# A graph network on one core: the last edge pass with masked scans in place of selection products

## The reference

```python
h = jnp.maximum(_layernorm(x, axis=-1), 0.0)
x = x + _L3_gnn_ref(h, edge_index, ...)

def _L3_gnn_ref(x, edge_index, W_e, b_e, W_n1, b_n1, W_n2, b_n2):
    src, dest = (edge_index[0], edge_index[1])
    edge_in = jnp.concatenate([x[src], x[dest]], axis=1)
    edge_attr = jax.nn.relu(edge_in @ W_e + b_e)            # 256 wide
    msg = jax.nn.relu(jnp.concatenate([x[dest], edge_attr], axis=1) @ W_n1 + b_n1)   # 256 wide
    agg = jax.ops.segment_sum(msg, dest, num_segments=x.shape[0])
    return jax.nn.relu(agg @ W_n2 + b_n2)                   # 128 wide
```

## Time and profile before

| | us |
|---|---|
| median of 3 runs | 3399.61 (3371.57 to 3420.72) |
| profiled execution, span from first to last instruction | 2778.5 |
| profiled execution, its own time | not listed apart from the three runs |
| `phase_mlp` in the span | from about 2110 to the end |

### The profile page before, as it was taken

The page is one execution under the profiler, slowest core; times in us unless marked ns, Lnnn a source line. Parts: engine busy times, 40 slices in busy tenths (PEclk is TensorE's granted clock), DMA queues, the critical chain, the costliest instruction groups (busy, mean ns, idle before and its releaser), DMA issues. The chain is left out here.

```text
span 2778.5 us, 52641 instructions
## 1 busy us (share of the span) xinstructions
PE 2088.4 (75%) x11015; PEld 1440.1 (52%) x11015; DVE 1937.7 (70%) x8744; ACT 1827.5 (66%) x4630; POOL 1430.0 (51%) x1442
## 2 busy tenths in 40 slices
PE   3376666676764888849884899566664999999996
PEld 1154444444443777748884544233332666666663
DVE  8687777777774777768885788688884555555552
ACT  4498888787884888869993343799992444444442
POOL 7777777777765666367770000000003566666663
PEclk9789988988897999979996999899997999999998
DMA  2355565565653666556661542799994222222220
GB/s 77 93 172 185 182 186 178 164 189 173 183 159 101 169 169 170 155 145 196 198 195 53 148 127 82 217 306 308 307 300 138 60 70 78 77 79 83 76 72 23
DMA packets 457630, 419.73 MB, mean 151 GB/s; under 512 B 56299, under 2 KB 353974, under 8 KB 457460
## 3 DMA queue, kind: packets, MB, share of 16 engines
q1 hardware_dynamic: 391028, 343.53, 40.5%
q0 software_dynamic: 64192, 74.09, 10.4%
q10 hardware_dynamic: 2240, 0.01, 0.0%
HBM read 236.96 MB, written 184.33 MB: 152 GB/s over the span
## 5 line engine op out<-in xcount | busy, mean ns | idle before, releaser
L2313 POOL DMA_INDIRECT mlp_bx<-t_X,k_bslot x2 | 2.0, 1016 | 609.0 <-POOLq L2579 608.7
L2329 POOL DMA_INDIRECT out_dram<-mlp_ou,mlp_iro x200 | 200.5, 1002 | 185.7 <-issue 185.4
L486 POOL DMA_INDIRECT second_xs<-t_X,second_irs x200 | 199.7, 999 | 126.9 <-ACT second_m L1227 50.8
L2322 POOL DMA_INDIRECT mlp_xs<-t_X,mlp_irs x200 | 202.5, 1012 | 72.9 <-issue 60.0
L486 POOL DMA_INDIRECT a_xs<-in_x_dram,a_irs x200 | 206.4, 1032 | 61.4 <-issue 58.8
L486 POOL DMA_INDIRECT first_rd<-t_R,a_irs x200 | 202.8, 1014 | 66.9 <-issue 59.7
L486 POOL DMA_INDIRECT project_xs<-t_X,project_irs x200 | 199.8, 999 | 65.8 <-issue 63.3
L2383 DVE TENSOR_TENSOR mlp_v<-mlp_ps_r,mlp_b 126x512 f32<-126x512 f32 x50 | 34.6, 692 | 243.0 <-ACT mlp_y L2442 233.2
L2205 PE MATMUL x_ps_o<-x_ht,x_wd 128*128 128x512 f32 (+1 forms) x198 | 115.8, 668 | 96.3 <-DVE x_ht L2105 79.7
L2485 PE MATMUL mlp_ps_e<-mlp_h,mlp_we 128*128 128x504 f32 x400 | 187.0, 590 | 1.3 <-ACT mlp_h L2464 1.3
L486 POOL DMA_INDIRECT a_xd<-in_x_dram,a_ird x152 | 159.0, 1046 | 52.3 <-issue 44.5
(11 more groups left out here) (400 smaller groups left out, 7011.5 us busy)
## 6 DMA issues: line engine op xcount, KB each, us to landing
t_X<-first_x SPq DMA_DIRECT2D x194, 256.0 KB, 3.4
first_x<-in_x_dram SPq DMA_DIRECT2D x97, 256.0 KB, 3.9
project_x<-t_X SPq DMA_DIRECT2D x97, 256.0 KB
x_x<-t_X SPq DMA_DIRECT2D x97, 256.0 KB, 4.3
t_X<-x_x SPq DMA_DIRECT2D x97, 256.0 KB, 4.3
out_dram<-x_ou SPq DMA_DIRECT2D x97, 256.0 KB, 4.7
t_G<-second_g SPq DMA_DIRECT2D x50, 267.8 KB
t_X<-first_xo SPq DMA_DIRECT2D x50, 252.0 KB
```

Source lines behind the costliest of these rows:

```text
L486: pool.indirect_dma_start(dst[:, q, :], None, table, bass.IndirectOffsetOnAxis(ap=idx[:, q:q + 1], axis=0)).then_inc(s_rows, 16)
L2322: pool.indirect_dma_start(Xs[u][:, q, :], None, T["X3"], bass.IndirectOffsetOnAxis(ap=irs[u][:, q:q + 1], axis=0)).then_inc(s_rows[u], 16)
L2329: pool.indirect_dma_start(out, bass.IndirectOffsetOnAxis(ap=iro[s][:, q:q + 1], axis=0), OU[s][:, q, :], None, bounds_check=N - 1, oob_is_ ...
```

## The change

In the last edge pass only. The destination rows are turned feature-major by a transpose, as the source rows are, and a backward scan on DVE (multiply by a mask that is 0 at a segment's last slot, then max with the value) spreads each row over its segment; it also does their Relu, since its initial value is 0. The last product is made feature-major, with 500 edges along the free axis. A forward scan (multiply by a mask that is 0 at a segment's first edge, then add) makes running sums, with the last column of the tile before as initial value. ScalarE adds bias and Relu, TensorE turns the rows back, and DVE adds `Xd`. The masks `fm` and `bm` are computed and stored in `phase_prep` and loaded by broadcast. S0 is no longer used in this phase and its memory is freed before it. On DVE, `indices` and `stats` of the next tile now stand before the scans, and the output of tile t-4 behind them; on ScalarE `root(t+1)` moves ahead. GpSimd's body is as before.

```diff
@@ phase_prep
+        sp.wait_ge(s_f, 5)
+        for b in range(2):
+            sp.dma_start(half(T["fm"], b), fm[:, b, :]).then_inc(s_rows, 16)
+            sp.dma_start(half(T["bm"], b), bm[:, b, :]).then_inc(s_rows, 16)
...
+        dve.tensor_scalar(fm[:, :, :], fl[:, :, :], -1.0, 1.0, ALU.mult, ALU.add)
+        done(dve.tensor_scalar(bm[:, :, :], tl[:, :, :], -1.0, 1.0, ALU.mult, ALU.add))
@@ phase_mlp, SyncE
-                if not before(t, 2):
-                    sp.wait_ge(s_sel, t - 1)
-                sp.dma_start(dr[r][:, :].rearrange("p (k j) -> p k j", k=GT),
-                             T["dr"][bass.ds(t * GT, GT), :].partition_broadcast(RW)).then_inc(s_dr[r], 16)
+                if not before(t, 2):
+                    sp.wait_ge(s_sp, t - 1)
+                sp.dma_start(bm[r][:, :].rearrange("p (k j) -> p k j", k=GT),
+                             T["bm"][bass.ds(t * GT, GT), :].partition_broadcast(128)).then_inc(s_bm[r], 16)
+                if not before(t, 4):
+                    sp.wait_ge(s_ys, t - 3)
+                sp.dma_start(fm[f][:, :].rearrange("p (k j) -> p k j", k=GT),
+                             T["fm"][bass.ds(t * GT, GT), :].partition_broadcast(128)).then_inc(s_fm[f], 16)
@@ phase_mlp, GpSimd, once before the loop
+        for i in range(2):
+            pool.memset(Yr[i][:, 0:1], 0.0).then_inc(s_pad, 1)
@@ phase_mlp, DVE
-        def select(t, v):
...
+        def summed(g, v):
+            if there(g, NGE):
+                r, f = v % 2, v % 4
+                dve.wait_ge(s_fm[f], landed(g, f, 4))
+                dve.wait_ge(s_y, g + 1)
+                if not before(g, 2):
+                    dve.wait_ge(s_yr, g - 1)
+                if not before(g, 1):
+                    dve.wait_ge(s_ys, g)
+                init = 0.0 if before(g, 1) else Ys[1 - r][:, E4 - 1:E4]
+                dve.tensor_tensor_scan(Ys[r][:, :], fm[f][:, :], psY[:, 0:E4], init, ALU.mult, ALU.add).then_inc(s_ys, 1)
+
+        def spread(t, v):
+            if there(t, NGE):
+                r = v % 2
+                dve.wait_ge(s_bm[r], landed(t, r, 2))
+                dve.wait_ge(s_t, t + 1)
+                if not before(t, 2):
+                    dve.wait_ge(s_m, 2 * (t - 1))
+                dve.tensor_tensor_scan(Hb[r][:, 1, ::-1], bm[r][:, ::-1], psH[1][:, 0:W4][:, ::-1], 0.0, ALU.mult, ALU.max).then_inc(s_sp, 1)
...
         def body(t, v):
             r, u = v % 2, v % 4
-            g, s = t - 4, u
-            if there(g, NGE):
-                dve.wait_ge(s_co, (g + 1) * GT)
-                if there(g + 1, NGE):
-                    dve.wait_ge(s_ci, (g + 1) * GT + 1)
...
-                dve.tensor_tensor(V[r][:, :, :], psR[0:RW, :].rearrange("p (q d) -> p q d", q=GT), b2[0:RW, :, :], ALU.add).then_inc(s_v, 1)
...
+            indices(t + 3, (u + 3) % 4)
+            stats(t + 1, (v + 1) % 8)
+            summed(t - 2, (v - 2) % 8)
+            spread(t, v)
+            g, s = t - 4, u
             if there(g, NGE):
                 if not before(g, 4):
                     dve.wait_ge(s_sc[s], landed(g - 4, s, 4, GT) + scattered[s])
                 dve.tensor_copy(iro[s][:, :], kp.sidx[:, bass.ds(g * GT, GT)]).then_inc(s_io, 1)
-                dve.wait_ge(s_v, g + 1)
-                dve.scalar_tensor_tensor(OU[s][:, :, :], V[r][:, :, :], 0.0, Xd[(v - 4) % 8][:, :, :], ALU.max, ALU.add).then_inc(s_o, 1)
-            indices(t + 3, (u + 3) % 4)
-            stats(t + 1, (v + 1) % 8)
-            select(t + 1, (v + 1) % 8)
+                dve.wait_ge(s_b, g + 1)
+                dve.tensor_tensor(OU[s][:, :, :], Xd[(v - 4) % 8][:, :, :], psR[0:RW, :].rearrange("p (q d) -> p q d", q=GT), ALU.add).then_inc(s_o, 1)
@@ phase_mlp, ScalarE
             attr(g1, r1, 0)
-            carry(g3, r3, 1)
...
             attr(g1, r1, 1)
-            carry(g3, r3, 3)
+            root(t + 1, 1 - r)
             if there(t, NGE):
                 act.wait_ge(s_t, t + 1)
...
+                act.activation(Hb[r][:, 0, :], psH[0][:, 0:W4], ACT.Relu).then_inc(s_h, 1)
+            if there(g2, NGE):
+                act.wait_ge(s_ys, g2 + 1)
+                if not before(g2, 2):
+                    act.wait_ge(s_b, g2 - 1)
+                act.activation(Yr[r2][:, 1:1 + E4], Ys[r2][:, :], ACT.Relu, bias=b2[:, 0:1]).then_inc(s_yr, 1)
             message(g1, r1, 0)
-            carry(g2, r2, 0)
-            root(t + 1, 1 - r)
             message(g1, r1, 1)
@@ phase_mlp, TensorE
             attr(g1, r1, 0)
-            sums(g3, r3, 0)
+            attr(g1, r1, 1)
...
-                for q in range(GT):
-                    for w in range(2):
-                        ins = pe.matmul(psY[0:RW, q * 128:(q + 1) * 128], Mb[r2][:, w, q * RW:(q + 1) * RW], wn2[:, w, :],
-                                        start=(w == 0), stop=(w == 1))
+                for w in range(2):
+                    ins = pe.matmul(psY[:, 0:E4], wn2[:, w, :], Mb[r2][:, w, :], start=(w == 0), stop=(w == 1))
...
                 for q in range(GT):
                     pe.transpose(psH[0][:, q * RW:(q + 1) * RW], Z[r][:, q, :], kp.ident[0:RW, 0:RW])
-                    ins = pe.matmul(psH[1][:, q * RW:(q + 1) * RW], Z[r][:, GT + q, :], kp.select(t, q), start=True, stop=True)
+                    ins = pe.transpose(psH[1][:, q * RW:(q + 1) * RW], Z[r][:, GT + q, :], kp.ident[0:RW, 0:RW])
                 ins.then_inc(s_t, 1)
-            sums(g3, r3, 3)
+            if there(g3, NGE):
+                pe.wait_ge(s_yr, g3 + 1)
...
+                for q in range(GT):
+                    ins = pe.transpose(psR[0:RW, q * 128:(q + 1) * 128], Yr[r3][:, q * EPT:q * EPT + RW], kp.ident[:, :])
+                ins.then_inc(s_b, 1)
             message(g1, r1, 0)
             message(g1, r1, 1)
```

More of the change, by code:

```diff
@@ L49 @@
 W4 = GT * RW
+E4 = GT * EPT
 EPS = 1e-5
@@ L294, in phase_prep @@
     bsf = sb("bsf", [HT, 2])
+    fm = sb("fm", [HT, 2, EPT])
+    bm = sb("bm", [HT, 2, RW])
     w1 = sb("w1", [128, 128])
@@ L2238, in phase_mlp @@
     Z = [sb(f"z{i}", [RW, 2 * GT, 128]) for i in range(2)]
-    dr = [sb(f"dr{i}", [RW, W4]) for i in range(2)]
+    fm = [sb(f"fm{i}", [128, E4]) for i in range(4)]
+    bm = [sb(f"bm{i}", [128, W4]) for i in range(2)]
     rt = [sb(f"rt{i}", [RW, GT]) for i in range(2)]
@@ L2342, in indices @@
                 dve.tensor_copy(irs[s][:, :], kp.idx[:, bass.ds(g * GT, GT)]).then_inc(s_idx, 1)
-        def select(t, v):
-            if there(t, NGE):
-                r = v % 2
-                dve.wait_ge(s_dr[r], landed(t, r, 2))
-                for q in range(GT):
-                    k = bass.ds(t * GT + q, 1)
-                    ins = dve.tensor_scalar(kp.select(t, q), dr[r][:, q * RW:(q + 1) * RW], kp.dcol[:, k], None, ALU.is_equal)
-                ins.then_inc(s_sel, 1)
         def stats(t, v):
@@ L2429, in message @@
                     act.wait_ge(s_y, g - 1)
-                act.activation(Mb[r][:, h, :], psM[h][:, 0:W4], ACT.Relu, bias=bn1[:, h:h + 1]).then_inc(s_mr, 1)
-        def carry(g, r, q):
-            if not there(g, NGE):
-                return
-            if q == 0:
-                act.wait_ge(s_ye, g + 1)
-            if before(g, 1) and q == 0:
-                act.activation(Y[r][0:1, q, :], kp.zrow[0:1, 0:128], ACT.Copy).then_inc(s_ci, 1)
-                return
-            act.wait_ge(s_co, g * GT + q)
-            o = 128 * ((q + GT - 1) % GT)
-            act.activation(Y[r][0:1, q, :], psR[0:1, o:o + 128], ACT.Copy).then_inc(s_ci, 1)
+                act.activation(Mb[r][:, h, :].rearrange("p (q e) -> p q e", q=GT),
+                               psM[h][:, 0:W4].rearrange("p (q e) -> p q e", q=GT)[:, :, 1:RW], ACT.Relu,
+                               bias=bn1[:, h:h + 1]).then_inc(s_mr, 1)
+        act.wait_ge(s_pad, 2)
         root(0, 0)
@@ L2498, in message @@
             ins.then_inc(s_m, 1)
-        def sums(g, r, q):
-            if not there(g, NGE):
-                return
-            if q == 0 and not before(g, 1):
-                pe.wait_ge(s_v, g)
-            pe.wait_ge(s_ci, g * GT + q + 1)
-            s0 = kp.select(g, q)
-            pe.matmul(psR[0:RW, q * 128:(q + 1) * 128], s0, Y[r][:, q, :], start=True, stop=True).then_inc(s_co, 1)
         def body(t, u):
@@ L2556, in gnn_kernel @@
         marks = []
-        with ExitStack() as early:
-            kp.ahead(Mem(nc, early, "a"))
-            run(nc, marks, phase_prep, kp, T, a)
-            run(nc, marks, phase_hist, kp, T, a)
-            run(nc, marks, phase_first, kp, T, a)
-        with ExitStack() as middle:
-            kp.later(Mem(nc, middle, "l"))
-            run(nc, marks, phase_second, kp, T, a)
-            with ExitStack() as some:
-                sx = Scores(Mem(nc, some, "s"))
-                run(nc, marks, phase_project, kp, T, a, sx)
-                run(nc, marks, phase_softmax, kp, T, a, sx)
-                run(nc, marks, phase_attend, kp, T, a, sx)
```

(17 more changed lines are left out.)

70 lines of the change are left out of this document (29 added, 41 removed).

## The result

The changed kernel takes 3538.68 us (median of four runs, 3535.09 to 3550.86) beside 3400.69 for the kernel before (four runs, 3371.57 to 3420.72): 1.042 times the time, with an interval of 1.036 to 1.047.

What follows compares the result with a forecast made beforehand. It took TensorE to bound the old kernel at 12.42 us a tile and a DVE/GpSimd circle of waits the new one at 18.35; 44 tiles, start and end added 244 to 3399.6, giving 3644 us, range 3590 to 3712.

Steps and rivals of the forecast that it cites:

- The ring: In the last phase, DVE's output, GpSimd's scatters and gathers, and DVE's next `stats` wait in a circle: 18.35 us per tile.
- T: The end of DVE's output instruction (L2402), from which times in a tile are counted; 12.85 us to the next `stats`.
- 44 steps: Steps from the last phase's first output at 2165.6 to 2712.2, 12.42 us each before, forecast at 18.35 each, 807.4 us.
- 44 P - 563.6: Forecast difference in us between changed and old kernel, with P the time per tile in the last phase.
- the filling: Start of the last phase before its first output, which was forecast at 2168 us in place of 2165.6.
- the tail: Part behind the last of the evenly spaced outputs: 33 us to the last scatter in place of 52.5, then 13.8 unchanged.
- A: Rival, chance 0.03: TensorE stays the bound in the last phase at 11.46 us a tile, 3352 us in all.
- B: Rival, chance 0.07: DVE's scans are as cheap as a copy, 17.2 us a tile, 3593 us in all.
- C: Rival, chance 0.10: gathers land later under the second mask (14.14 us), or scans take 2.0 each; 3701 or 3710 us.
- the fit: DVE scan times extrapolated from shorter scans in the trace: 1.22 us for 504 columns, 1.27 for 500 with pointer.
- D: Rival, chance 0.05: TensorE runs at the low clock for whole tiles, 22.9 us each, and becomes the bound; 3844 us.
- Its milder half: A tile with its first 7 us slow costs TensorE 3.5 us, within 7 of slack; the time stays as forecast.

Runs made afterwards that it cites:

- `after_out_first`: The changed kernel with DVE's index copy and output of tile t-4 moved back to the front of the body: 3324.22 us, 0.977 of the kernel before.

## Why the prediction was right, and where it failed

**The mechanism was right, and in its size.** The ring and its terms, on the long kind that was to be forecast: T to `stats` 12.94 in the tile shown and 12.75 to 13.33 in all (forecast 12.85), `stats` and aggregates 2.35 (2.36), scans 2.23 (2.35), index copy and output 0.73 (0.80), in all 18.25 in that tile and 18.23 on the mean (18.35). DVE idle for 10.0 before `stats` (some 9), GpSimd for 7.94 before the first scatter (some 8). Undone alone, the ring took the slowdown with it (3324.22); made alone in the kernel before, it slowed that one (3460.97).

**The step that failed is the base of the sum**: "The median of the runs shown is 3399.6, 621 above the span, which holds what lies around it; I leave that as it is". Nothing had shown that 621 us lie around a span. It was a difference between a profile of one kind of execution and times of another. In the timed kind the old tile took 14.67 and not 12.42, so 44 steps cost 156.6 and not 44 x (18.35 - 12.42) = 260.9. The formula "44 P - 563.6" carries the same error. With 14.67 in place of 12.42 it gives 44 x 3.68 = 162 and, with the forecast's own ends (2.4 in the filling, -19.4 in the tail), 145; the medians differ by 138. That these two are so near is in part luck, since the ends were wrong too: in the two profiled runs of the long kind they came to +6.0 and +7.0, and the spans differ by 169.7. What stands ahead of the prediction makes the same mistake, where it explains the 621 us by what lies before the first and after the last instruction; that part is 1.5 us.

**The tail was mis-sized, by 24 us**, which the short kind shows, where everything else is as in the profile read. There the 44 steps cost 257 (260.9 forecast) and the filling -2.7 (+2.4), but from the last output of the ring to the end of the span it takes 72.0 where it took 67.0: +5.0 against -19.4. The prediction let the last tile's path and GpSimd's six groups of scatters run in 33 us, from the ring's last output to the last scatter; in the run of the changed kernel on the short kind that takes 57.1 (2966.4 to 3023.5). The next three outputs still come 15.7, 12.9 and 12.2 us apart, because the turns back wait for the output of the tile before, as in the second ring of 14, with some passes at the low clock. The last three outputs then come within 3.5 us, and GpSimd needs 15.2 for their scatters, 5.2 a tile as forecast.

**TensorE's place in the ring was wrong as well**, at no cost to the period. The prediction had its turns back at T + 5.3, `message` until T + 10.8 and then 7 us idle, all of it slack. In the trace the turns back wait for the output and begin at T + 0.15, and the turns of Z, the last work of the tile, end at T + 14.5, some 2 us before the backward scan takes them.

**The rivals.** A (TensorE the bound at 11.46) needed a gather ahead of the scatter and, as it turned out, the output ahead of the scans or the turns behind `message` as well; built so, it is true to 0.02 us on the short kind. B and C fall by the scans, 1.23 and 1.18 (1.27 and 1.22 by the fit), and by a landing of 12.94 under two masks. D as priced, the low clock for the whole tile (22.9 us), did not come. Its milder half did, slow passes early in the tile that cost the period nothing: TensorE is busy 593/44 = 13.48 us a tile in place of 11.46, so they add 2.0 where 3.5 were counted, and the run with less TensorE work stays at 18.20. TensorE's share of 74% busy where I had forecast 62% is that clock, not more work.

**Not shown:** what makes an execution short or long, and what makes waits end late in the long kind. It goes with the indirect DMAs in this phase; that it does so in `phase_first` and the others was read from windows only, and the same test was not tried there. Nor was `after_out_first` run in the short kind.

## What to carry to other kernels

Before a difference is added to a measured time, compare the time with the span of the profile: here the span of after lies 1.5 us under its time, and a gap of 621 meant that profile and times were of different executions. When an instruction that waits for a DMA is moved ahead of one that releases the next DMA, write the ring out and divide by the tiles that it spans: the same terms that make 18.2 us over one tile would make 9.1 a tile over two (an estimate from the terms above), and with the output in front and the scatter one tile later TensorE's 11.48 was what remained. Ask also what the other engines wait for: an engine can be idle for 4.7 us in a tile and yet have only some 2 to spare. And a kernel whose bounding engine is full has no slack for late waits, so its gain or loss can depend on them.

## What had not been expected of the hardware

The same program ran in 2779 or in 3292 to 3400 us, with engines busy as long as before in the last phase and waits between them ending up to some 10 us late: 14.67 us a tile in place of 12.42 in the batch of 3400, with eight indirect DMAs per tile. In the batch of 3292 the outputs were 12.42 apart with two indirect DMAs per tile, and 13.90 and uneven in the other profiled kernel, with eight. There was no difference in the phase without any (358 and 357 us). The spread may go with it: in that batch 51 us over the thirteen runs of the kernel before and 4 us over the four with few indirect DMAs. The cause is open.
